# A fused three-layer kernel: full-height first maxima, another order of the maxima in a step, and a PSUM copy moved from ScalarE to VectorE

## The chip, the cores and the metric

The kernel runs on one NeuronCore of a Trainium2 chip as one launch. The metric is the device time of that launch in microseconds. Before the change the median of three runs is 1235.82 us (1234.45 to 1237.55).

## What is computed

Three residual layers on x, of shape 4 x 256 x 256; nearly all of the time goes into the first. It is a cross-attention of x (256 queries a batch) over a context of 4096 rows of 192 values a batch, with 16 heads of 16 columns:

```
q = (layernorm(x) @ Wq + bq)   -> [4, 16 heads, 256, 16]
k = (context @ Wk + bk)        -> [4, 16 heads, 4096, 16]
v = (context @ Wv + bv)        -> [4, 16 heads, 4096, 16]
attn = softmax(clip(q k^T * 16**-0.5, -10000, 10000))
x = x + (attn @ v) @ Wo + bo
```

Then follow a causal self-attention with normed keys and queries, and a layer that routes tokens to 64 slots. Both lie behind the code that the change touches.

## The kernel before, in words

**Groups, steps, units.** The cross-attention runs over 16 groups q of four heads each (four groups a batch). A group has 64 units, one `[128, 512]` PSUM bank each. Four units are a step, one for each head j = 0 to 3, so a group has 16 steps, numbered 0 to 15 here. A unit has two jobs that are far apart in time. Its maximum (`max_unit`, L1708) multiplies a stationary tile of 128 queries by 512 keys, and VectorE reduces the bank to a column (`reduce_unit`, L1173). Its scores (`score_half`, L1722, two products of 256 columns) are key rows by 256 queries; ScalarE takes their exponential (L982). Maxima run AHEAD = 76 units before scores, since the shift of the softmax must be known.

**Split operands.** A product takes only 51 of the array's 128 rows: 16 head columns of keys or queries twice, once more for the low part, and three rows (32 to 34) of ones against the shift in three parts. The even head of a pair lies on partitions 0 to 50 (row half 0), the odd one on 64 to 114 (row half 64). The context's projections in the loop (`passes`, L1674, nine products of 256 columns per half chunk, the first four on row half 64, the last five on row half 0) take 64 rows. Operands on different row halves can be worked on side by side.

**Rings.** Scores use three banks `st` (with two `low` bounds at step 0 and the turned shift behind step 14 in the same ring), maxima use three banks `mxb` (`mx0`, `mx1`, `misc`), with the sums of the last group (`finish`) once a group in the same ring. A user of a ring waits for the release of the user three places before.

**TensorE's order in a step (L1869 on).** Written out by hand: scores of head 0 with two passes, maximum 0, two passes, scores of head 2 with maxima 1 and 2 in and behind them, scores of head 1, a pass, maximum 3, a pass, scores of head 3 with passes. Behind them come, where due, `spread_low` (t = 3), `turn_shift` (t = 59), `values` (L1762: 16 products of 17 columns on four column groups, for the step before), and `finish` (t = 7).

**The other engines' order.** VectorE reduces one maximum a unit; at t = 8 and 9 it takes the reciprocal of the sums and normalises them (`take_sums`, `normalise`); at t = 52 to 60 `shift_step` makes the next group's shift. ScalarE takes one exponential a unit, the bounds at t = 3 (L902), and copies key and value chunks out of `kps`, a half chunk at a time: `k_first_half` (L867), `v_copy_half` (L887), both behind the third exponential of a step; at t = 59 it copies the turned shift (`shift_rows`, L895). POOL splits the context and the keys in two parts (L704, L706, L657, L659), and reads a flag at the head of each group, clears rows of `qst` (L747) and branches; `clip_done`, on which `values` waits, is set behind the branch. SyncE issues the loads of key blocks (L444, L446), queries, context, and the writes of keys.

**The lead.** Before the loop, TensorE computes 20 key chunks and 17 value chunks with full-height products (L1570; 128 rows, then 65 rows), the queries (L1634) and turns of the input (L1622), as 62 `filling`s. Six of them come first, the rest lie between the first 76 maxima, two maxima at a time, with two banks in turn. Keys go through kscr in DRAM: ScalarE copies a chunk, POOL splits it, SyncE writes it, ScalarE's queue loads it back (`load_first`). The rows of ones in the key ring `kst` come from two memsets of VectorE (L1129) and four DMAs of SyncE (`ones_rows`).

```
            for n in range(0, AHEAD, 2):
                max_unit(n)
                max_unit(n + 1)
                filling(fill(n))
                filling(fill(n + 1))
```

Of the kernel before, what the change touches and what calls it, by code (L numbers as in the profile page):

```python
# [31 lines left out]
RB = 12  # L32
NX = 12
# [8 lines left out]
def build(nc, a, out):  # L42

    with ExitStack() as ctx:
# [63 lines left out]

        low = sb("low", [P, 4, T])
# [219 lines left out]
        def fill(m):  # L329

            return m - m // 6 + 6 if m % 6 < 5 else None

        def after_fill(f):

            return f - 6 + (f - 6) // 5 + 2
# [14 lines left out]
        def mx_free(eng, kind, n):  # L350

            place = mx_place[kind, n] - 3 if (kind, n) in mx_place else None
            if place is None:
                wait(eng, max_red, n - 1)
            elif place == -1:
                eng.wait_ge(shift_set, 2)
                eng.wait_ge(flag_abs, 1)
            elif place < 0:
                eng.wait_ge(max_red, AHEAD + place + 2)
            else:  # L360
                user, m = mx_users[place]
                if user == "max":
                    eng.wait_ge(max_red, m + 1)
                else:
                    eng.wait_ge(head_out, 2 * (m + 1))

# [83 lines left out]
        def _(sp):  # L450
# [9 lines left out]
            def ones_rows():  # L460

                sp.wait_ge(ones_set, 2)
                for r in (32, 96):
                    one = kst[r:r + 3, 0:1, 0:512].bitcast(F32)
                    sp.dma_start(kst[r:r + 3, 0, 512:RB * 512].bitcast(F32).rearrange("p (n q) -> p n q", q=512),
                                 one.to_broadcast([3, RB - 1, 512])).then_inc(ones_set, 16)
                    sp.dma_start(kst[r:r + 3, 1, :].bitcast(F32).rearrange("p (n q) -> p n q", q=512),
                                 one.to_broadcast([3, RB, 512])).then_inc(ones_set, 16)

# [39 lines left out]
            def load_q(q):  # L509
# [4 lines left out]
                if 1 <= q < 3:  # L514
                    sp.wait_ge(qst_in, 64 * q)
# [15 lines left out]
            ones_rows()  # L531
# [3 lines left out]
            write_k(2)  # L535
            load_q(0)
# [13 lines left out]
            sp.wait_ge(stacks_in[3], 128)  # L550
            for n in range(8, 10):
                load_block(n)
# [81 lines left out]
        def _(pool):  # L634
# [103 lines left out]
            for q in range(NQ):  # L738
                pool.wait_ge(flag_set, q + 1)
                clipping = pool.value_load(flag[0:1, 0:1])  # L740
                if q > 0 and q + 2 < NQ:
# [6 lines left out]
                    pool.wait_ge(zero_set, 2 * q)  # L748
# [78 lines left out]
        def _(act):  # L827
# [93 lines left out]
            def load_first(n):  # L921

                act.wait_ge(*written(2 * n))
# [45 lines left out]
            act.wait_ge(rows_set, 8)  # L969
# [7 lines left out]
            for n in range(NU):  # L977
# [10 lines left out]
                if t % 4 == 2:  # L988
# [135 lines left out]
        def _(dve):  # L1124
# [3 lines left out]
            for r in (32, 96):  # L1128
                dve.memset(kst[r:r + 3, 0, 0:512].bitcast(F32), 1.0).then_inc(ones_set, 1)  # L1129
# [3 lines left out]
            dve.wait_ge(rows_set, 4)  # L1133
# [32 lines left out]
            def reduce_unit(n):  # L1166
# [5 lines left out]
                at = mxp[:, q % 2, m % 4, m % 8 // 4, m // 8:m // 8 + 1]  # L1172
                dve.reduce_max(at, bank_of_max(n)[:, :], AX.X).then_inc(max_red, 1)  # L1173

            def shift_step(q, t):
# [26 lines left out]
                elif t == 59:  # L1202
# [4 lines left out]
                elif t == 60:  # L1207
# [27 lines left out]

            def sums(q):
# [78 lines left out]
            for n in range(NU):  # L1315
# [245 lines left out]
        def _(pe):  # L1561
# [134 lines left out]
            def max_unit(n):  # L1696

                q, m = n // UQ, n % UQ
                if m == 0:
                    pe.wait_ge(qst_in, 64 * (q + 1))  # L1700
                    if q > 2:
                        pe.wait_ge(zero_set, 2 * (q - 2))
# [3 lines left out]
                j, qt, at = m % 4, m % 8 // 4, n // 8 % RB * 512  # L1706
# [147 lines left out]
            for f in range(6):  # L1854
                filling(f)
            pe.wait_ge(rows_set, 8)
            pe.wait_ge(ones_set, 2 + 16 * 4)
# [413 lines left out]
```

## Time and profile before

| | |
|---|---|
| runs, median | 1235.82 us |
| the profiled execution, its own time | 1235.44 us |
| its span, first to last instruction | 1233.7 us |
| mean granted TensorE clock | 0.935 |
| busy: TensorE / VectorE / ScalarE / POOL | 89% / 64% / 61% / 30% |
| chain that ended last: TensorE / VectorE / ScalarE | 64% / 18% / 5% |

The 1.7 us between own time and span lie outside the instructions. The clock is given as a share of 2.4 GHz; 0.50 is 1.2 GHz. Busy shares overlap and are means over stages: the lead (0 to 156 us), the loop (156 to some 1050 us) and the two later layers (to the end).

### The profile page before, as it was taken

What the parts mean: (1) busy time and instruction counts of PE and PEld (TensorE: products, weight loads), DVE (VectorE), ACT (ScalarE), POOL (GpSimd) and SP (SyncE); (2) the same over time, 40 slices, a digit from 0 to 9 for tenths busy, and PEclk for the clock granted to TensorE, in tenths of its full rate; (3) what the DMA queues carried; (4) which work ended last, traced back from release to release, by engine and by line L of the source; (5) the groups of instructions that cost most, each with busy time, mean ns of one, the idle gap of its engine ahead of it and who ended that gap; (6) DMA issues with size and microseconds to landing.
All of it is one profiled execution on the core that took longest, in us unless ns stands there. A gap on an engine that the chain in (4) does not pass through costs nothing.

```text
span 1233.7 us, 29233 instructions
## 1 busy us (share of the span) xinstructions
PE 1099.1 (89%) x11517; PEld 709.2 (57%) x11521; DVE 791.7 (64%) x1499; ACT 750.1 (61%) x1429; POOL 373.6 (30%) x438
## 2 busy tenths in 40 slices
PE   7899888899898989989898988989889888987997
PEld 6566465565565556555555655555555554555655
DVE  3334577577777877777787777766776612594553
ACT  2111278587777878777787877765766746324432
POOL 4422355344444444444344433140000000202320
PEclk9658899899999999999999999987997989998999
DMA  8731654344454445445444444222342000000001
GB/s 205 233 111 42 190 170 144 116 141 144 128 159 135 135 141 147 134 142 150 132 145 130 148 143 120 63 66 74 104 125 58 25 27 2 1 1 2 3 1 35
DMA packets 117032, 128.66 MB, mean 104 GB/s; under 512 B 19955, under 2 KB 91126, under 8 KB 116864
## 3 DMA queue, kind: packets, MB, share of 16 engines
q1 hardware_dynamic: 111392, 120.29, 33.0%
q10 hardware_dynamic: 5472, 6.23, 2.1%
q8 instruction: 93, 1.52, 0.5%
q14 instruction: 75, 0.61, 0.2%
HBM read 88.42 MB, written 37.75 MB: 102 GB/s over the span
## 4 chain that ended last, share of the span: by engine, by line
PE 64%; DVE 18%; issue 9%; ACT 5%; DMA 2%; SPq 1%; ACTq 0%; POOLq 0%; POOL 0%; DVEq 0%
PE acc L1762 19%; DVE mxp L1173 12%; PE st L1722 12%; PE mx L1708 9%; PE misc L1708 4%; PE st L1570 3%; PE kps L1674 2%; DVE free_k L1408 2%; PE acc L1570 2%; ACT prob L982 1%; PE setB L2022 1%; PE kps L1570 1%; ACT prob L1070 1%; DMA kscr<-o_sb 1%; PE mx L1565 1%
## 5 line engine op out<-in xcount | busy, mean ns | idle before, releaser
L1173 DVE TENSOR_REDUCE mxp<-mx 128x1 f32<-128x512 f32 x709 | 465.6, 683 | 219.4 <-PE mx L1708 219.4
L982 ACT ACTIVATE prob<-st 128x512 f32<-128x512 f32 x704 | 385.7, 598 | 157.9 <-PE st L1722 157.1
L1722 PE MATMUL st<-qst,kst 51*128 51x256 f32 x2048 | 398.1, 304 | 9.1 <-ACT prob L982 8.8
L1722 PEld LDWEIGHTS st<-qst,kst 51*128 51x128 f32 x2048 | 316.0, 192 | 127.0 <-issue 76.8
L1708 PE MATMUL mx<-kst,qst 51*128 51x512 f32 x709 | 282.0, 457 | 47.5 <-DVE mxp L1173 31.5
L1173 DVE TENSOR_REDUCE mxp<-misc 128x1 f32<-128x512 f32 x315 | 215.1, 683 | 64.2 <-PE misc L1708 64.2
L982 ACT ACTIVATE xn<-st 128x512 f32<-128x512 f32 x320 | 176.5, 598 | 56.4 <-PE st L1722 55.7
L1762 PE MATMUL acc<-prob,v_raw 128*17 128x256 f32 x2816 | 196.2, 398 | 9.4 <-issue 5.4
L1708 PEld LDWEIGHTS mx<-kst,qst 51*128 51x128 f32 x709 | 131.3, 194 | 114.3 <-DVE mxp L1173 85.0
L1708 PE MATMUL misc<-kst,qst 51*128 51x512 f32 x315 | 137.6, 437 | 22.8 <-DVE mxp L1173 14.9
L1674 PE MATMUL kps<-w_hi,ctx_p 64*128 64x256 f32 x564 | 153.5, 315 | 0.0
L1674 PE MATMUL kps<-ctx_p,w_hi 64*128 64x256 f32 x528 | 144.5, 314 | 5.9 <-POOL ctx_p L706 5.9
L706 POOL TENSOR_TENSOR ctx_p<-ctx,ctx_p 128x512 fp32r<-128x512 f32 x91 | 116.8, 1284 | 7.3
L1762 PEld LDWEIGHTS acc<-prob,v_raw 128*17 128x17 f32 x2816 | 67.8, 98 | 71.5 <-issue 14.2
L704 POOL CAST ctx_p<-ctx 128x512 fp32r<-128x512 f32 x91 | 55.5, 610 | 146.6 <-PE kps L1674 146.5
L1674 PEld LDWEIGHTS kps<-w_hi,ctx_p 64*128 64x128 f32 x564 | 99.0, 188 | 0.0
L657 POOL CAST kraw<-kraw 128x512 fp32r<-128x512 f32 x50 | 30.6, 612 | 220.9 <-ACT kraw L867 196.6
L1674 PEld LDWEIGHTS kps<-ctx_p,w_hi 64*128 64x128 f32 x528 | 91.4, 186 | 6.2 <-POOL ctx_p L706 6.2
L1762 PE MATMUL acc<-xn,v_raw 128*17 128x256 f32 x1280 | 87.4, 391 | 1.8 <-ACT prob L982 1.4
L1708 PEld LDWEIGHTS misc<-kst,qst 51*128 51x128 f32 x315 | 59.7, 189 | 46.5 <-DVE mxp L1173 38.1
L1674 PE MATMUL kps<-w_lo,ctx_p 64*128 64x256 f32 x282 | 76.3, 284 | 0.0
L1674 PE MATMUL kps<-ctx_p,w_lo 64*128 64x256 f32 x264 | 70.0, 279 | 0.0
(424 smaller groups left out, 1256.5 us busy)
## 6 DMA issues: line engine op xcount, KB each, us to landing
kst<-kscr SPq DMA_DIRECT2D x240, 128.0 KB, 2.5
kscr<-kraw SPq DMA_DIRECT2D x100, 256.0 KB, 2.6
kst<-kscr SPq DMA_DIRECT2D x240, 64.0 KB, 2.6
ctx<-in_ctxT SPq DMA_DIRECT2D x93, 128.0 KB, 2.6
ctx<-in_ctxT SPq DMA_DIRECT2D x184, 64.0 KB, 2.4
kscr<-prob SPq DMA_DIRECT2D x16, 256.0 KB, 3.6
kscr<-o_sb SPq DMA_DIRECT2D x12, 256.0 KB, 4.1
qscr<-v_raw SPq DMA_DIRECT2D x8, 256.0 KB, 2.5
```

The lines of the kernel that those rows point to most:

```text
L657: pool.tensor_copy(first.bitcast(F32R), full).then_inc(k_1, 1)
L704: pool.tensor_copy(hi, raw).then_inc(part_step, 1)
L706: pool.tensor_tensor(lo, raw, hi.bitcast(F32), ALU.subtract).then_inc(part_step, 1)
L982: act.activation(exps(unit_at(n)), st_bank("scores", unit_at(n))[:, :], ACT.Exp).then_inc(exp_done, 1)
L1070: act.activation(pexp[n % 3], setB[:, :, 0:3 * P], ACT.Exp).then_inc(a_exp, 1)
L1173: dve.reduce_max(at, bank_of_max(n)[:, :], AX.X).then_inc(max_red, 1)
L1408: dve.tensor_reduce(amax[:, 2 * b + qt, :, r], bank[:, :, qt * P:(2 * qt + 1) * P], AX.X, ALU.max, negate=True).then_inc(a_max, 1)
L1570: return pe.matmul(to, weights, moving, start=start, stop=stop)
L1674: mm = pe.matmul(kps[:, g * CH:(g + 1) * CH], ctx_part[:, col] if m else w_part[:, col], w_part if m else ctx_part, start=(i == 0), stop=( ...
L1708: pe.matmul(bank_of_max(n)[:, :], qst[row, 2 * (q % 3) + j // 2, qt * P:(qt + 1) * P], kst[row, j // 2, at:at + 512], start=True, stop=Tru ...
L1722: mm = pe.matmul(st_bank("scores", n)[:, h * T:(h + 1) * T], kst[row, j // 2, at:at + P], qst[row, 2 * (q % 3) + j // 2, :], start=True, s ...
L1762: mm = pe.matmul(acc[32 * j:32 * j + VW, 0:T], v4[:, q // 4 % 2 * 32 + n, h, :], exps(UQ * q + 4 * (n // 2) + j)[:, n % 2 * T:(n % 2 + 1) ...
```

## The change

It has these parts:

- **First maxima.** The 64 maxima of group 0 multiply a new tile `qz` (four heads, each on its own rows, zeros on all others) by all 128 rows of the key ring, instead of 51 rows by 51. SyncE loads `qz` with four DMAs ahead of `load_q(0)`; the first maximum waits for both. All rows 32 to 63 and 96 to 127 of the ring are set to one by memsets: four of VectorE in two parts, two of POOL behind key chunk 7. The four DMAs and two small memsets of before are gone; `load_first` waits for the memsets.
- **Fillings.** Eight instead of six come before the first maximum.
- **Order of a step.** The first maximum comes first, the second behind the scores of head 0 and a pass, the third between the halves of head 1, the fourth behind the scores of head 3. The maxima take the heads in the order 1, 0, 2, 3.
- **Value copies.** VectorE makes the second half's copy of each value chunk of the loop, at t % 8 = 6 behind its reduction; ScalarE keeps the first.
- **Ends of groups.** `values` comes ahead of `turn_shift`; `shift_rows` moves to t = 60, behind that exponential, the flag's two steps to t = 60 and 61; `take_sums` and `normalise` both to t = 7.

```diff
@@ helpers @@
+            return (1, 0, 2, 3)[m % 4]          (head_of_max)
@@ sync, behind write_k(2) @@
+            sp.wait_ge(qscr_w, 64)
+            sp.wait_ge(rows_set, 5)
+            for e in range(2):
+                heads_of = qz[:, :, :].rearrange("p (i e) t -> p i e t", e=2)[:, :, e, :]
+                sp.dma_start(heads_of[64 * e:64 * e + 32, :, :].bitcast(F32), ...)
+                sp.dma_start(heads_of[64 * e + 35:64 * e + HR, :, :].bitcast(F32), ...)
             load_q(0)
@@ gpsimd @@
                 k_split(c)
+                if c == 7:
+                    pool.wait_ge(k_2, 8)
+                    for r in (32, 96):
+                        pool.memset(kst[r:r + 32, :, 8 * 512:RB * 512].bitcast(F32), 1.0).then_inc(zero_set, 1)
+                    pool.wait_ge(zero_set, 2)
@@ scalar @@
-                    if c is not None:
-                        v_copy_half(c, t % 8 // 4)
-                if t == 59 and q + 1 < NQ:
+                    if c is not None and t % 8 < 4:
+                        v_copy_half(c, 0)
+                if t == 60 and q + 1 < NQ:
                     shift_rows(q + 1)
@@ vector @@
+            dve.memset(qz[:, :, :].bitcast(F32), 0.0).then_inc(rows_set, 1)
+            def ones_rows(first, end):
+
+                for r in (32, 96):
+                    dve.memset(kst[r:r + 32, :, first * 512:end * 512].bitcast(F32), 1.0).then_inc(ones_set, 1)
...
+            ones_rows(0, 4)
             dve.wait_ge(q_1, 1)
             dve.tensor_tensor(q_sb[:, :, 0:T], ...).then_inc(q_2, 1)
+            ones_rows(4, 8)
...
+                if t % 8 == 6 and v_job(q, t // 8) is not None:
+                    v_copy_half(v_job(q, t // 8))
-                if t == 8 and q > 0:
+                if t == 7 and q > 0:
                     take_sums(q - 1)
-                if t == 9 and q > 0:
                     normalise(q - 1)
@@ tensor, max_unit @@
+                if n < UQ:
+                    pe.matmul(bank_of_max(n)[:, :], qz[:, j, qt * P:(qt + 1) * P], kst[:, j // 2, at:at + 512],
+                              start=True, stop=True).then_inc(max_ps, 1)
+                    return
@@ tensor, a step @@
+                    if more:
+                        max_unit(n + AHEAD)
                     score_half(n, 0)
-                    next(some, None)
                     score_half(n, 1)
                     next(some, None)
                     if more:
-                        max_unit(n + AHEAD)
+                        max_unit(n + 1 + AHEAD)
                     next(some, None)
                     next(some, None)
                     score_half(n + 2, 0)
-                    if more:
-                        max_unit(n + 1 + AHEAD)
+                    next(some, None)
                     score_half(n + 2, 1)
+                    score_half(n + 1, 0)
                     if more:
                         max_unit(n + 2 + AHEAD)
-                    score_half(n + 1, 0)
                     score_half(n + 1, 1)
+                    next(some, None)
+                    score_half(n + 3, 0)
+                    next(some, None)
+                    score_half(n + 3, 1)
                     next(some, None)
                     if more:
                         max_unit(n + 3 + AHEAD)
                     next(some, None)
-                    score_half(n + 3, 0)
-                    next(some, None)
-                    next(some, None)
-                    score_half(n + 3, 1)
                     next(some, None)
...
+                if n >= 7 and t % 4 == 3:
+                    values((n - 7) // UQ, (n - 7) % UQ // 4)
                 if t == 59 and q + 1 < NQ:
                     turn_shift(q + 1)
-                if n >= 7 and t % 4 == 3:
-                    values((n - 7) // UQ, (n - 7) % UQ // 4)
```

## Rows read from the trace of the kernel before

**Rows 1.** Chain that ended last, a steady step: start us, us, engine and line

```profile
503.96 0.70 DVE mxp L1173
...
504.70 0.39 PE mx L1708
...
505.44 0.99 PE acc L1762 x16
...
508.62 0.99 PE acc L1762 x16
```

**Rows 2.** Timeline, the same step: start us, us, engine, instruction, [idle before <-releaser]

```profile
503.18 0.39 PE L1722 MATMUL st<-qst,kst 51*128 51x256 f32 x1
503.40 0.28 PE L1722 MATMUL st<-qst,kst 51*128 51x256 f32 x1
503.52 0.40 PE L1708 MATMUL mx<-kst,qst 51*128 51x512 f32 x1
503.72 1.59 ACT L982 ACTIVATE prob<-st 128x512 f32<-128x512 f32 x3 [0.54 <-PE st L1722]
505.16 0.28 PE L1674 MATMUL kps<-ctx_p,w_lo 64*128 64x256 f32 x1
505.37 1.06 PE L1762 MATMUL acc<-prob,v_raw 128*17 128x256 f32 x16
505.88 0.59 ACT L982 ACTIVATE prob<-st 128x512 f32<-128x512 f32 x1
```

**Rows 3.** Timeline, the step behind `finish`

```profile
551.55 0.35 DVE L1252 TENSOR_TENSOR o_sb<-mx,rcp 128x64 f32<-128x64 f32 x2
551.95 0.50 PE L1708 MATMUL mx<-kst,qst 51*128 51x512 f32 x1 [1.48 <-DVE o_sb L1252]
551.95 0.50 PE L1722 MATMUL st<-qst,kst 51*128 51x256 f32 x2
```

**Rows 4.** Timeline, the products of `finish` in five groups

```profile
493.45 0.63 PE L1565 MATMUL mx<-ident,accs 128*32 128x128 f32 x16
548.94 0.52 PE L1565 MATMUL mx<-ident,accs 128*32 128x128 f32 x12
602.72 0.64 PE L1565 MATMUL misc<-ident,accs 128*32 128x128 f32 x16
821.26 0.62 PE L1565 MATMUL mx<-ident,accs 128*32 128x128 f32 x16
883.30 0.62 PE L1565 MATMUL mx<-ident,accs 128*32 128x128 f32 x16
```

**Rows 5.** Busy time in stretches: last three columns clock, DMA share, GB/s

```profile
45.00:104.00 59.00, 59.00 (x141) 37.42 (x141) 22.89 (x37) 7.98 (x14) 14.20 (x15) 0.50 0.37 114
106.00:141.00 35.00, 34.51 (x143) 22.97 (x142) 19.62 (x31) 9.74 (x17) 9.25 (x13) 1.00 0.36 101
```

**Rows 6.** Chain that ended last, in the lead, before the clock rose

```profile
99.38 3.71 PE misc L1634 x8
103.09 1.65 PE st L1622 x8
```

**Rows 7.** Timeline, the end of a group

```profile
538.14 1.20 ACT L895 ACTIVATE qst<-st 3x512 fp32r<-3x512 f32 x2
...
541.08 0.61 POOL L704 CAST ctx_p<-ctx 128x512 fp32r<-128x512 f32 x1 [2.51 <-PE kps L1674]
```

**Rows 8.** Timeline, the next group's first `values`

```profile
548.08 1.06 PE L1762 MATMUL acc<-prob,v_raw 128*17 128x256 f32 x16 [0.43 <-ACT xn L982]
```

**Rows 9.** Groups by line: VectorE's copies of a full bank out of PSUM

```profile
L1163 DVE COPY xnT<-st x2: 681/681/681, 95.6 to 113.3; 128x512 f32<-128x512 f32 x2
```

**Rows 10.** Timeline, memsets and the queue's issues in the lead

```profile
6.29 1.34 DVE L1136 MEMSET qst<- 3x1536 f32 x1 [0.27 <-issue]
...
19.77 0.69 DVE L1261 TENSOR_TENSOR v_raw<-v_raw 128x512 f32<-128x512 f32 x1 [8.42 <-ACT v_raw L937]
...
30.41 0.42 SPq L517 DMA_DIRECT2D qst<-qscr  x1
...
42.22 2.90 PE L1570 MATMUL acc<-v_raw,wk 128*128 128x256 f32 x8 [1.79 <-ACT prob L859]
```

More of the change, by code:

```diff
@@ L32 @@
 RB = 12
+F0 = 8
 NX = 12
@@ L107, in ctx_of @@
             return ctx4[:, late_slot[c], :, :]
+        first_q = ctx.enter_context(ExitStack())
+        qz = first_q.enter_context(nc.sbuf_tensor("qz", [P, 4, T], F32R))
+        first_q.close()
         low = sb("low", [P, 4, T])
@@ L329, in fill @@
         def fill(m):
-            return m - m // 6 + 6 if m % 6 < 5 else None
+            return m - m // 6 + F0 if m % 6 < 5 else None
         def after_fill(f):
-            return f - 6 + (f - 6) // 5 + 2
+            return f - F0 + (f - F0) // 5 + 2
         def bank_of_max(n):
@@ L365, in mx_free, with head_of_max @@
                     eng.wait_ge(head_out, 2 * (m + 1))
+        def head_of_max(m):
+            return (1, 0, 2, 3)[m % 4]
         def unit_at(n):
@@ L458, in load_early @@
                              a["ctxT"][first:end, P:C, :].rearrange("c p t -> p c t")).then_inc(ctx_in[n], 16)
[L460 to L468, printed above, removed]
             def load_ctx(slot, c):
@@ L514, in load_q @@
                 if 1 <= q < 3:
-                    sp.wait_ge(qst_in, 64 * q)
+                    sp.wait_ge(qst_in, 64 * (q + 1))
                 for e in range(2):
@@ L530, in _ @@
             load_early(4, 8, 3)
-            ones_rows()
             write_k(0)
@@ L535, in _ @@
             write_k(2)
+            sp.wait_ge(qscr_w, 64)
+            sp.wait_ge(rows_set, 5)
+            for e in range(2):
+                heads_of = qz[:, :, :].rearrange("p (i e) t -> p i e t", e=2)[:, :, e, :]
+                sp.dma_start(heads_of[64 * e:64 * e + 32, :, :].bitcast(F32),
+                             qscr1[0:64, :, 0:T].rearrange("(i e d) r t -> e (d r) i t", i=2, e=2)[e]).then_inc(qst_in, 16)
+                sp.dma_start(heads_of[64 * e + 35:64 * e + HR, :, :].bitcast(F32),
+                             qscr2[0:64, 0:T].rearrange("(i e d) t -> e d i t", i=2, e=2)[e]).then_inc(qst_in, 16)
             load_q(0)
@@ L550, in _ @@
             sp.wait_ge(stacks_in[3], 128)
+            sp.wait_ge(zero_set, 2)
             for n in range(8, 10):
@@ L747, in _ @@
                         pool.memset(qst[r:r + 3, to:to + 2, :].bitcast(F32), 0.0).then_inc(zero_set, 1)
-                    pool.wait_ge(zero_set, 2 * q)
+                    pool.wait_ge(zero_set, 2 + 2 * q)
                 with pool.If(clipping != 0):
@@ L921, in load_first @@
             def load_first(n):
+                act.wait_ge(ones_set, 2 if n < 4 else 4)
                 act.wait_ge(*written(2 * n))
@@ L968, in _ @@
                 k_first(c)
-            act.wait_ge(rows_set, 8)
+            act.wait_ge(rows_set, 9)
             shift_rows(0)
@@ L1127, in _ @@
             dve.memset(early[C2:C2 + 1, 0:3, CH:2 * CH], 1.0).then_inc(rows_set, 1)
-            for r in (32, 96):
-                dve.memset(kst[r:r + 3, 0, 0:512].bitcast(F32), 1.0).then_inc(ones_set, 1)
             dve.memset(wv[C2:C2 + 1, 1, :], 0.0).then_inc(rows_set, 1)
+            dve.memset(qz[:, :, :].bitcast(F32), 0.0).then_inc(rows_set, 1)
             dve.memset(shrow[:, :].bitcast(F32), 0.0).then_inc(rows_set, 1)
             dve.memset(spad[:, :, :, :], 0.0).then_inc(rows_set, 1)
-            dve.wait_ge(rows_set, 4)
+            dve.wait_ge(rows_set, 5)
             for r in (32, 96):
@@ L1171, in reduce_unit @@
                 dve.wait_ge(max_ps, n + 1)
-                at = mxp[:, q % 2, m % 4, m % 8 // 4, m // 8:m // 8 + 1]
+                at = mxp[:, q % 2, head_of_max(m), m % 8 // 4, m // 8:m // 8 + 1]
                 dve.reduce_max(at, bank_of_max(n)[:, :], AX.X).then_inc(max_red, 1)
@@ L1201, in shift_step @@
                                       ALU.subtract).then_inc(m_3, 1)
-                elif t == 59:
+                elif t == 60:
                     dve.wait_ge(shift_ps, q + 1)
@@ L1206, in shift_step @@
                                       apply_absolute_value=True).then_inc(flag_abs, 1)
-                elif t == 60:
+                elif t == 61:
                     dve.wait_ge(flag_abs, q + 1)
@@ L1234, in centre_weights, with v_copy_half @@
                                          ALU.mult, ALU.add).then_inc(kq_c, 1)
+            def v_copy_half(c):
+                dve.wait_ge(v_ps, v_steps(c) + 2)
+                dve.wait_ge(v_out, v_steps(c) + 1)
+                if c >= 32:
+                    dve.wait_ge(pv_done, 16 * (4 * (c // 16 - 1) - 1) + c % 16 + 1)
+                dve.tensor_copy(v4[:, 2 * c % 64 + 1, :, 0:DH], kps[:, D:2 * D].rearrange(
+                    "p (h d) -> p h d", d=DH)).then_inc(v_out, 1)
             def sums(q):
@@ L1699, in max_unit @@
                 if m == 0:
-                    pe.wait_ge(qst_in, 64 * (q + 1))
+                    pe.wait_ge(qst_in, 64 * (q + 2))
                     if q > 2:
-                        pe.wait_ge(zero_set, 2 * (q - 2))
+                        pe.wait_ge(zero_set, 2 + 2 * (q - 2))
                 if n % 8 == 0:
@@ L1705, in max_unit @@
                 mx_free(pe, "max", n)
-                j, qt, at = m % 4, m % 8 // 4, n // 8 % RB * 512
+                j, qt, at = head_of_max(m), m % 8 // 4, n // 8 % RB * 512
+                if n < UQ:
+                    pe.matmul(bank_of_max(n)[:, :], qz[:, j, qt * P:(qt + 1) * P], kst[:, j // 2, at:at + 512],
+                              start=True, stop=True).then_inc(max_ps, 1)
+                    return
                 row = slice(64 * (j % 2), 64 * (j % 2) + HR)
@@ L1852, in filling @@
                     early_k(16 + (f - 54) // 2, f % 2)
-            for f in range(6):
+            for f in range(F0):
                 filling(f)
-            pe.wait_ge(rows_set, 8)
-            pe.wait_ge(ones_set, 2 + 16 * 4)
+            pe.wait_ge(rows_set, 9)
             for n in range(0, AHEAD, 2):
```

## The prediction, as put on record before the run

> **What bounds the kernel now.** I read the chain of waits first, since the shares of busy time say little: TensorE is 89% busy, but not at its peak. In a steady step of the loop the chain goes through one reduction of VectorE and the maximum that it releases, then through the products of `values` [rows 1]: VectorE reduces the step's first maximum (0.70 us), only then is a bank free for the fourth (504.70), and `values` ends the step. `values` recurs after 3.18 us [rows 1], mostly 3.17, and does so in 10 or 11 of the 16 steps of every group. The loop is thus held by a round trip, not by an engine: four reductions of 0.68 us a step leave VectorE idle.
>
> The timeline of the same step gives what a forecast needs [rows 2]. I set the step's start at 0 (503.18). The second half of the first scores starts at 0.22, the first maximum at 0.34; other products follow each other on their row half at 0.12 us for 256 columns, 0.23 for 512. ScalarE starts 0.32 after the second half of the scores started, and takes 0.60 for one exponential. `values` starts 0.21 behind the last pass, and the next step 0.99 behind that.
>
> Two more things stand out. Behind `finish`, a maximum waits 1.48 us for the sums to be normalised [rows 3]. And the granted clock is at its low level (0.50, 1.2 GHz) in most of the lead, from 45 to 104 us, with TensorE busy all the time: 0.42 us an instruction there, 0.24 in the stretch behind it with the same mix at 2.4 GHz [rows 5]. The last thing before it rose was the queries and turns, all on 128 rows, 5.4 us without a maximum between [rows 6]; the rounds before, with 51-row maxima and 65-row products in between, had left it low.
>
> **The steady step, worked out again with the new order.** Start 0: first maximum (row half 64) beside the first scores (row half 0). The trace has such a pair, both starting at 551.95 [rows 3]. Second half of the scores 0.22; pass and second maximum 0.34; passes 0.46, 0.57; scores of head 2 0.57 and 0.69; head 1 0.81, with the third maximum beside it, and 0.92; a pass 1.04. The first half of head 3 needs the bank of the first scores: exponential from 0.54 (0.22 + 0.32) to 1.14, release at 1.19 (the row of a released maximum shows 0.04 us). So it starts at 1.19, not 1.04; its second half, after a stop, 0.22 later, at 1.41; fourth maximum 1.53 (its bank is free at 1.27: the first maximum lands at 0.49, reduction to 1.22); last pass 1.64; `values` 1.85; next step 2.84. That is 0.33 less than 3.17. VectorE needs four starts at 0.60, 2.4 us, and ScalarE's last exponential ends 1.31 behind the last pass started (the distance of 505.16 to 506.47 in [rows 2]), at 2.95, before the next step's first scores are there (3.38). The batches without projections have the same path and get the same.
>
> The copy on VectorE, 256 columns from PSUM: bounds are 0.17 (64 columns, half of the pair of 0.35, [rows 3]) and 0.68 (a copy of 512 columns, [rows 9]). I take 0.4, between the ends by its columns. It falls between the third and fourth reduction of one step in four and fills idle time of VectorE (2.8 of 2.84 us then); cover gone, it costs what it takes over, at most 0.3 us on 47 steps, 14 us. What it relieves on ScalarE was hidden.
>
> **Group by group.** From one `finish` to the next is 53.78 us where the clock stays up (548.94 to 602.72, [rows 4]).
> - Ten full steps at -0.33: -3.3.
> - The step behind `finish`: VectorE now has reciprocal and both products (about 0.6 us) right behind the sums, and the third maximum, which uses their bank, comes at 0.81. The 1.48 goes, and a little more: -1.6.
> - Step 13 gains 0.4, step 14 0.3: VectorE's seven small operations of the shift (about 1.4 us in two steps) now delay it.
> - Step 15 loses. The third scores use the bank of the turned shift. Before, ScalarE copied it (1.20 us, [rows 7]) ahead of the step's exponentials, and nothing stood. Now the copy is queued behind the first exponential (ends 1.14), so it ends at 2.36 and the third scores start at 2.41 instead of 0.81. `values` comes at 3.41: +1.4.
> - Steps 0 and 1: nothing. From the last pass of step 15, POOL splits a chunk (541.08, [rows 7]), loads the flag, clears rows and branches, which no busy row shows, and `values` of step 1 waits for it to 548.08 [rows 7, 8]. These 7.0 us hold before and after the change; TensorE's own work in that stretch is some tenths shorter by the distances above (two steps and the two bounds).
>
> Sum: -3.3 - 1.6 - 0.7 + 1.4 = -4.2 a group. Fifteen groups have it (the last has no maxima): -62, with the first, which has no `finish`, 1.6 less: -61.
>
> **Low clock inside the loop.** Groups with such an episode are longer: 55.49 (493.45 to 548.94, [rows 4]), one of five by about 1.7 us, and two of the later ones without projections by about 8: 62.04 (821.26 to 883.30, [rows 4]). Together some 24 us. They began right behind the 1.48 us stop at `finish`. That stop goes, but step 15 gets one as long (0.97 to 2.41, last product landed to next start). So I let three quarters of them stay: -6.
>
> **The lead.** A maximum costs TensorE the same with 51 rows as with 128, if columns set it as they do for the projections' 128 and 65 rows. What can change is the clock. With 128-row maxima no product in these rounds is lower than 65 rows. I expect the clock to rise some ten us into the rounds, at 55 instead of 104. 49 us at 0.42 an instruction become 29 at 0.245 [rows 5]: -20. The bounds are 0 (as before) and -25 (up at once).
> The Trainium skill (TensorE: Matmul & The Clock Gate, Part 1) lets the clock follow how busy the engine has been. The trace disagrees: 59.00 of 59.00 us busy at 0.50. By that rule alone the rows would change nothing, which is the first rival.
>
> Against it: SyncE issues four more loads ahead of `write_k(3)`, 1.9 us at 0.42 each [rows 10], and ScalarE's queue, then chunk 7's copy, then the filling at 42.22 [rows 10] wait for that write: +2. The two fillings moved ahead only move the stop there. Memsets: by 1.34 us for 1536 columns VectorE needs 14 us for 4 x 4096; half of it falls where it was idle for 8.42 us [rows 10], half between that product and the statistics of the other tokens, with some us to spare. POOL needs, at the same rate, 7 us behind chunk 7, which delays chunks 8 and 9, first read by the 33rd maximum. Both at nothing; cover gone, 7 us. SyncE loses four DMAs ahead of its first write, at most 0.4. So the lead gives -18.
>
> **Sum.** -61 - 6 - 18 = -85. The profiled execution's own time is 1235.4 (1.7 over its span), the median 1235.8; so 1151.
>
> **Rivals.**
> 1. The lead's clock stays low (the rows don't matter). For: nothing in the trace shows a 128-row maximum. The loop's gain stays: 1235.8 - 67 + 2 = 1171.
> 2. Another wait takes the reduction's place. The exponential's round trip already is the next limit (1.19 against 1.04). If ScalarE or VectorE is late by some tenths a step (the value copy, an exponential that starts behind its predecessor), the step is 3.0 and the group's gain halves: -32 - 3 - 18, 1183.
> 3. Slower: the maximum at the head of the step, and the one at its end, do not run beside products of the other row half, since nothing in the trace shows one right behind `values` or right ahead of it. Then the first scores start 0.34 later and the passes behind the fourth maximum 0.22: step 3.40, +0.23 each. A group gets 11 x 0.23 - 1.5 + 1.6 = +2.6, fifteen +39; with the lead's -18, 1257. It decides from a step of 3.3 us on. Against: [rows 3], both starting at once.
>
> **Chances.** Forecast (1125 to 1168) 0.50, rival 1 0.22, rival 2 0.20, rival 3 0.08, of which some 0.03 end within 0.3% (what a measurement of this kernel can tell from no change). The forecast's low end is all of the low-clock episodes gone (-18 more) and the lead at its -25. The range goes to 1198, past rivals 1 and 2 and a value copy without cover. Faster 0.92, same 0.03, slower 0.05.
>
> **What would show it.** Right: `values` every 2.84 us in steady steps, with idle time ahead of the fourth scores released by ScalarE, none ahead of the fourth maximum; no wait on the normalising; in step 15 the third scores 1.6 us late behind L895's copy; `finish` to `finish` 49.6 us; clock 1.00 from about 55 us, and the first `values` at about 144 instead of 162 us. Wrong: a step near 3.2 with first scores behind the first maximum; 0.50 up to 100 us; or `kps` passes late behind VectorE's copy.

## The result, and the profile of the changed kernel

Four runs of the changed kernel gave a median of 1132.93 us (1130.69 to 1140.26), four of the kernel before beside them 1235.13 (1227.62 to 1237.55): ratio 0.9192, 95% interval 0.9135 to 0.9250. The profiled execution took 1132.47, span 1130.7, so 103 us less than the profiled one of before, where 85 were forecast. Some executions of any version run at a lower clock and take some per cent longer; the ranges below include them, the ratios don't.

The page of the changed kernel: TensorE's busy share has risen from 89% to 92%, and the row of its granted clock has fewer dents. Section 5 has a new wait, of `scores` for the shift copy; maxima hardly wait for VectorE.

```profile
PE 1043.2 (92%) x11521; PEld 718.0 (63%) x11521; DVE 825.7 (73%) x1549; ACT 712.5 (63%) x1382; POOL 380.7 (34%) x440
...
PEclk9899599999999999999999999979999899999999
...
L1754 PE MATMUL st<-qst,kst 51*128 51x256 f32 x2048 | 409.9, 311 | 31.5 <-ACT qst L906 22.4
...
L1740 PE MATMUL mx<-kst,qst 51*128 51x512 f32 x645 | 267.8, 436 | 1.8 <-DVE mxp L1189 1.5
```

**A steady step.** Timeline of the changed kernel, against [rows 2]. L1740 is the maximum, L1754 the scores, L1702 the passes, L1794 `values`, L994 the exponential, L1258 the new copy on VectorE.

```profile
496.70 0.50 PE L1740 MATMUL misc<-kst,qst 51*128 51x512 f32 x1
496.70 0.50 PE L1754 MATMUL st<-qst,kst 51*128 51x256 f32 x2
...
497.04 0.39 PE L1740 MATMUL mx<-kst,qst 51*128 51x512 f32 x1
...
497.93 0.39 PE L1754 MATMUL st<-qst,kst 51*128 51x256 f32 x1
...
498.27 0.39 PE L1740 MATMUL misc<-kst,qst 51*128 51x512 f32 x1
...
498.60 1.06 PE L1794 MATMUL acc<-prob,v_raw 128*17 128x256 f32 x16
499.58 0.50 PE L1740 MATMUL mx<-kst,qst 51*128 51x512 f32 x1
```
```profile
497.28 2.06 ACT L994 ACTIVATE prob<-st 128x512 f32<-128x512 f32 x4 [0.54 <-PE st L1754]
```
```profile
499.04 0.41 DVE L1258 COPY v_raw<-kps 128x256 f32<-128x256 f32 x1
```

The first maximum and the first scores start together at 496.70. The fourth scores start 1.23 later (forecast 1.19), their second half and the fourth maximum follow at once, `values` comes at 1.90 (1.85), the next step at 2.88 (2.84). It was 3.17. The new copy falls into idle time of VectorE, 0.41 us at 499.04.

**Behind `finish`** (L1593) nothing stops, and from one `finish` to the next are 49.82 us, against 53.78 in [rows 4]:

```profile
493.25 0.63 PE L1593 MATMUL mx<-ident,accs 128*32 128x128 f32 x16
493.82 0.49 PE L1740 MATMUL mx<-kst,qst 51*128 51x512 f32 x1
...
543.07 0.64 PE L1593 MATMUL misc<-ident,accs 128*32 128x128 f32 x16
```

**Step 15** has the new wait. First exponential, shift copy (L906), and only then the third scores, 2.45 behind the step's start at 531.54:

```profile
531.54 0.50 PE L1754 MATMUL st<-qst,kst 51*128 51x256 f32 x2
532.12 0.60 ACT L994 ACTIVATE prob<-st 128x512 f32<-128x512 f32 x1 [0.76 <-PE st L1754]
532.74 1.20 ACT L906 ACTIVATE qst<-st 3x512 fp32r<-3x512 f32 x2
533.99 0.38 PE L1754 MATMUL st<-qst,kst 51*128 51x256 f32 x1 [1.47 <-ACT qst L906]
```

**The lead.** Busy time in stretches (columns as in [rows 5]), then the chain in a cycle of rounds:

```profile
38.90:45.70 6.80, 6.18 (x15) 4.94 (x16) 1.29 (x2) 2.06 (x4) 6.07 (x4) 0.50 1.03 270
45.70:114.00 68.30, 64.66 (x292) 51.91 (x290) 44.90 (x73) 17.74 (x31) 30.43 (x32) 1.00 0.52 152
114.00:137.90 23.90, 18.12 (x93) 11.58 (x95) 13.83 (x28) 8.89 (x17) 13.07 (x15) 0.50 0.68 211
```
```profile
49.82 0.86 PE kps L1598 x4
50.68 0.87 PE acc L1598 x4
51.55 0.47 PE mx L1736 x2
...
54.02 0.69 DVE mxp L1189
```

The clock rises at 45.7 instead of 104. At the end of the lead, where TensorE has stops (18.12 us busy of 23.90), it falls again, from 114.0 to 137.9; before, it did so for 13.7 us from 145.5. The first `values` start at 134.2 (before 162.4). VectorE's reduction is on the chain in the rounds here, as it was not between 43 and 104 us before: with the clock up, TensorE catches up with the two-bank ring.

### The profile page after: what moved, and what is told of

Read it like the earlier page. It is cut to its first block, busy times and chain, and to the rows that moved or that the text cites. A ratio compares the mean times of both kernels' runs of the same rounds, so it can differ in the third digit from the quotient of the medians.

```text
span 1130.7 us, 29261 instructions
## 1 busy us (share of the span) xinstructions
PE 1043.2 (92%) x11521; PEld 718.0 (63%) x11521; DVE 825.7 (73%) x1549; ACT 712.5 (63%) x1382; POOL 380.7 (34%) x440
## 4 chain that ended last, share of the span: by engine, by line
PE 76%; issue 7%; DVE 7%; ACT 7%; DMA 1%; POOL 1%; SPq 1%; ACTq 0%; POOLq 0%; DVEq 0%
PE acc L1794 21%; PE st L1754 16%; PE mx L1740 9%; PE kps L1702 8%; PE misc L1740 5%; DVE free_k L1436 2%; PE st L1598 2%; ACT prob L994 2%; ACT qst L906 1%; PE mx L1736 1%; PE setB L2053 1%; ACT prob L1082 1%; DVE mxp L1189 1%; PE acc L1598 1%; PE mx L1593 1%
## 5 line engine op out<-in xcount | busy, mean ns | idle before, releaser
L994 ACT ACTIVATE prob<-st 128x512 f32<-128x512 f32 x704 | 377.1, 600 | 152.7 <-PE st L1754 152.2
L1754 PE MATMUL st<-qst,kst 51*128 51x256 f32 x2048 | 409.9, 311 | 31.5 <-ACT qst L906 22.4
L1754 PEld LDWEIGHTS st<-qst,kst 51*128 51x128 f32 x2048 | 299.4, 190 | 66.9 <-ACT qst L906 25.5
L1740 PE MATMUL mx<-kst,qst 51*128 51x512 f32 x645 | 267.8, 436 | 1.8 <-DVE mxp L1189 1.5
L994 ACT ACTIVATE xn<-st 128x512 f32<-128x512 f32 x320 | 172.2, 600 | 56.8 <-PE st L1754 56.4
L1794 PE MATMUL acc<-prob,v_raw 128*17 128x256 f32 x2816 | 193.9, 394 | 9.2 <-issue 5.4
L1740 PEld LDWEIGHTS mx<-kst,qst 51*128 51x128 f32 x645 | 122.9, 191 | 69.1 <-issue 35.9
L1740 PE MATMUL misc<-kst,qst 51*128 51x512 f32 x315 | 135.6, 430 | 0.0
L1702 PE MATMUL kps<-ctx_p,w_hi 64*128 64x256 f32 x528 | 129.2, 311 | 4.9 <-POOL ctx_p L717 4.9
L1702 PE MATMUL kps<-w_hi,ctx_p 64*128 64x256 f32 x564 | 132.5, 301 | 0.0
L1794 PEld LDWEIGHTS acc<-prob,v_raw 128*17 128x17 f32 x2816 | 66.1, 98 | 75.7 <-issue 12.7
L1702 PEld LDWEIGHTS kps<-w_hi,ctx_p 64*128 64x128 f32 x564 | 104.7, 186 | 2.1
L1702 PEld LDWEIGHTS kps<-ctx_p,w_hi 64*128 64x128 f32 x528 | 100.7, 192 | 7.3 <-POOL ctx_p L717 5.2
L1794 PE MATMUL acc<-xn,v_raw 128*17 128x256 f32 x1280 | 85.5, 385 | 2.1 <-ACT prob L994 2.1
L1740 PEld LDWEIGHTS misc<-kst,qst 51*128 51x128 f32 x315 | 59.4, 189 | 32.8 <-issue 16.2
L1702 PE MATMUL kps<-w_lo,ctx_p 64*128 64x256 f32 x282 | 74.4, 278 | 0.0
L1702 PE MATMUL kps<-ctx_p,w_lo 64*128 64x256 f32 x264 | 71.0, 283 | 0.0
```

What stands on the lines that cost most here:

```text
L994: act.activation(exps(unit_at(n)), st_bank("scores", unit_at(n))[:, :], ACT.Exp).then_inc(exp_done, 1)
L1702: mm = pe.matmul(kps[:, g * CH:(g + 1) * CH], ctx_part[:, col] if m else w_part[:, col], w_part if m else ctx_part, start=(i == 0), stop=( ...
L1740: pe.matmul(bank_of_max(n)[:, :], qst[row, 2 * (q % 3) + j // 2, qt * P:(qt + 1) * P], kst[row, j // 2, at:at + 512], start=True, stop=Tru ...
L1754: mm = pe.matmul(st_bank("scores", n)[:, h * T:(h + 1) * T], kst[row, j // 2, at:at + P], qst[row, 2 * (q % 3) + j // 2, :], start=True, s ...
L1794: mm = pe.matmul(acc[32 * j:32 * j + VW, 0:T], v4[:, q // 4 % 2 * 32 + n, h, :], exps(UQ * q + 4 * (n // 2) + j)[:, n % 2 * T:(n % 2 + 1) ...
```

## The experiments

Five questions: what in the lead makes the 28 us, what the order of the steps is worth, what step 15's wait costs, whether the copy on VectorE gains anything, and whether the exponential's round trip really sets the step. The kernel before ran beside each set of kernels: 1230.08 us for the first, 1237.15 for the second, 1239.19 for the third.

**1. The rows alone: first maxima back to 51 rows.**

```diff
-                if n < UQ:
-                    pe.matmul(bank_of_max(n)[:, :], qz[:, j, qt * P:(qt + 1) * P], ...)
-                    return
```

> The changed kernel, but its first 64 maxima multiply 51 rows by 51 again (the loads of qz, the memsets and the eight fillings stay). Theory (the array's height in use decides over the clock in the lead, and a change between 51-row and 128-row products costs TensorE some 0.2 us each way round): the clock stays at 0.50 up to about 100 us, the first values move from 134 back to about 160 us, time about 1160. Rival (the rows do nothing, the lead was shortened by the fillings and by the DMAs that went): first values at about 136, time within 3 us of 1133. Second rival (clock not touched, only the changes between heights cost): low stretch as short as now, first values 5 us later, 1138.

Measured: 1162.16 us (1157.96 to 1170.15), ratio 0.9452 (0.9367 to 0.9537). The first `values` are back at 161.1, so the rows carry 27 of the lead's 28 us. Busy time in two stretches, and a cycle of the lead at full clock:

```profile
39.30:93.90 54.60, 53.58 (x125) 33.73 (x126) 20.16 (x32) 8.15 (x14) 23.89 (x20) 0.50 0.46 142
```
```profile
116.97 0.50 PE L1736 MATMUL mx<-kst,qst 51*128 51x512 f32 x2
117.40 2.00 PE L1598 MATMUL st<-wv,v_raw 128*128 128x256 f32 x8
119.33 0.51 PE L1736 MATMUL mx<-kst,qst 51*128 51x512 f32 x2
...
123.58 0.50 PE L1736 MATMUL mx<-kst,qst 51*128 51x512 f32 x2
```

TensorE is busy 53.58 of 54.60 us and stays at 0.50 (1.2 GHz); with 128-row maxima in the same places it rose at 45.7. The second fence shows what I had not seen: between two pairs of 51-row maxima, eight filling products take from 117.40 to 119.33, 1.93 us. Eight filling products take 0.86 + 0.87 = 1.73 in the changed kernel (chain above, also at full clock). Six maxima with their twenty filling products take 6.61 here (116.97 to 123.58) and 6.04 there (61.84 to 67.88). So 128 rows are cheaper even where the clock is the same. Two things change together in this experiment: the rows of the maxima, and the changes between heights that 51-row maxima bring. The runs do not tell which of the two kept the clock low.

```profile
61.84 0.50 PE L1736 MATMUL mx<-kst,qz 128*128 128x512 f32 x1
```

The Trainium skill (TensorEngine Tiling (Array Packing), Key Properties) says that a change of tiling mode drains TensorE. The trace agrees, with the 0.2 us above; that it is a drain is the page's word, and the runs show only that the time goes where the heights change.

**2. Only the first sixteen maxima on 128 rows.**

```diff
-                if n < UQ:
+                if n < 16:
```

> The changed kernel with 128-row products for the first 16 maxima only, the other 48 of group 0 on 51 rows. Theory (full height is needed to raise the clock, not to hold it: the kernel of before held 1.00 from 105 us on with 51-row maxima; and every change between the heights costs about 0.2 us): the low stretch ends at about 46 us as in the changed kernel and does not come back before the last maxima; eight cycles of six maxima cost 0.55 more each, first values at about 138, time about 1137. Rival (full height is also needed to hold it): the clock falls again at some 60 us, first values above 150, time above 1148.

Measured: 1150.52 us (1135.82 to 1181.43), ratio 0.9292 (0.9067 to 0.9518). First `values` at 141.2, 7 later than with all 64. The clock was up through the 51-row maxima that followed:

```profile
62.00:119.00 57.00, 56.15 (x237) 37.47 (x236) 33.01 (x52) 14.76 (x26) 19.18 (x23) 1.00 0.46 136
```

So 16 maxima on 128 rows were enough for the rise here, and the 51-row maxima behind them did not end it. (Between 50.7 and 54.1, still among the sixteen, the clock was low once more, behind a stop of 2.41 us.) The 48 other maxima pay by the height changes: 48 / 6 x 0.57 = 4.6 of the 7 us. The time is further off than 7 us because two late groups of this profiled run had 17 and 31 us of low clock (from 743.6 and 798.2 on), which the lead's rows don't touch.

**3. Six fillings ahead instead of eight.**

```diff
-F0 = 8
+F0 = 6
```

> The changed kernel with six fillings ahead of the maxima, as before the change. Theory (TensorE stands ahead of the filling of chunk 9 whatever was put in front of it, as ScalarE's queue waits for a key write): first values within 2 us of 134, time 1133 to 1136. Rival (the two fillings ahead keep the clock up or shorten the lead): a longer low stretch and first values at 138 or later, 1138 and up.

Measured: 1137.08 us (1129.75 to 1151.98), ratio 0.9226 (0.9085 to 0.9366), first `values` at 135.6 against 134.2. The two fillings move a stop and save nothing that can be measured.

**4. The order alone, in the kernel before** (order of a step and of the heads in it, nothing else).

```diff
+                    if more:
+                        max_unit(n + AHEAD)
                     score_half(n, 0)
-                    next(some, None)
...
```

> The kernel of before with the new order of a step and of the heads, nothing else. Theory: steady steps of 2.88, the stop behind finish stays at about 1.5 us, the end of a group costs what it did, lead as before (first values at 162): 1235 - 48 = about 1187, give or take 6 for stretches of low clock. Rival (VectorE's copy and the order need each other): steps of 3.0 or more, 1205 and up.

Measured: 1160.44 us (1158.83 to 1165.46), ratio 0.9425 (0.9353 to 0.9498): 27 us better than expected. Steady steps are 2.88, so the order makes the whole of that gain. The step behind `finish` stays at 4.65, as it must with the sums taken a unit later; step 14 is 3.72 and step 15 2.93, 0.9 less than the changed kernel's 2.88 + 4.68. A group takes 50.4, 3.4 less than before: 51 us in fifteen. The first `values` come 4 us earlier (158.2). The rest, some 15 us, fits the low clock: 131 us of it in the whole profiled run where before had 162, and at half speed the difference is 15. I had priced only the steps.

**5. The old order, in the changed kernel.**

```diff
-                    if more:
-                        max_unit(n + AHEAD)
                     score_half(n, 0)
+                    next(some, None)
...
```

> The changed kernel with the step's order of before (maxima between, heads 0, 1, 2, 3); all else as changed. Theory (a step was held by the round trip first maximum, reduction, fourth maximum): steady steps go back from 2.88 to 3.17 us, 11 in each of 15 groups, +48: about 1181, and the wait of the fourth maximum for the reduction is back. The lead stays at 134 us. Rival (the order is worth little, the moved copy of values and the ends of groups freed the step): steps below 3.0, time below 1150.

Measured: 1193.48 us (1185.76 to 1201.27), ratio 0.9677 (0.9596 to 0.9758). Steady steps 3.17, first `values` at 135.9. Step 15 is 4.51, so its loss belongs to ScalarE's new queue order and not to the step's. The timeline shows the reduction's wait again, in each steady step:

```profile
496.69 0.49 PE L1740 MATMUL misc<-kst,qst 51*128 51x512 f32 x1 [0.19 <-DVE mxp L1189]
```

The median lies 12 us above the expected 1181. I had counted the steady steps alone: with those behind `finish` and at the end, a group is 3.6 us longer by its steps, 54 in fifteen. The low clock of its profiled run adds up to 107 us where the changed kernel has 77, which is 15 at half speed. Together that is 69, and the two profiled runs lie 69 apart (1201.27 and 1132.47).

**6. The shift copy one unit earlier on ScalarE.**

```diff
-                if t == 60 and q + 1 < NQ:
+                if t == 59 and q + 1 < NQ:
                     shift_rows(q + 1)
```

> The changed kernel with ScalarE's copy of the turned shift one exponential earlier, at t = 59 as before the change; values stay ahead of the turn. Theory (step 15 stands because that copy is queued behind the first exponential): the third scores of step 15 start at about 1.3 instead of 2.4 us, but the first exponential is 0.7 later and the fourth scores wait for it: step 15 from 4.68 to about 3.9, 15 times, -12: about 1121, with fewer stretches of low clock. Rival (ScalarE now stands waiting for the turn, which values precede, and holds the exponential of head 3 and the next step): no gain or a loss, 1130 to 1145.

Measured: 1115.53 us (1109.79 to 1119.00), ratio 0.9074 (0.9004 to 0.9145); once more, on another chip:

> shift_copy_t59 once more, on the same chip as turn_first_early, since the two are to be compared: step 15 at 3.86, about 1116 us. If it comes out within 0.3% of turn_first_early, the turn's place is worth nothing beside the copy's.

1115.79 us (1108.72 to 1120.56), ratio 0.9069 (0.8989 to 0.9149). The ten runs of the two lie below all four of the changed kernel. Step 15 in the timeline:

```profile
523.78 0.50 PE L1754 MATMUL st<-qst,kst 51*128 51x256 f32 x2
523.88 1.21 ACT L906 ACTIVATE qst<-st 3x512 fp32r<-3x512 f32 x2 [0.30 <-PE st L1767]
525.33 0.35 PE L1754 MATMUL st<-qst,kst 51*128 51x256 f32 x1 [0.58 <-DVE flagf L1221]
```

The third scores start 1.55 behind the step's start instead of 2.45. They wait for the copy and for VectorE's flag reduction, which reads the same bank. The step is 3.86 instead of 4.68; 0.8 x 15 is 12 us, and 17 were gained: the low clock in its first profiled run adds up to 39 us against 77 (in the other run to 77 as well). Only the part between the first `values` and the last group can come from step 15: there it is 8 and 23 us in these two runs and 38 in the changed kernel. Over all profiled runs with the stop of step 15 in them (the changed kernel, 1, 2, 3, 5, 8 and 9) it is 28 to 85 us there; in the four with the copy at t = 59 (these two and those of experiment 7) it is 7 to 23. This version beats both kernels.

**7. The turn of the shift ahead of the last `values`, too.**

```diff
-                if n >= 7 and t % 4 == 3:
-                    values((n - 7) // UQ, (n - 7) % UQ // 4)
                 if t == 59 and q + 1 < NQ:
                     turn_shift(q + 1)
+                if n >= 7 and t % 4 == 3:
+                    values((n - 7) // UQ, (n - 7) % UQ // 4)
```

> The changed kernel with the turn of the shift ahead of values and its copy at t = 59 again, as before the change. Theory (step 15 pays the queued copy, step 14 the wait for VectorE's small operations; with the new order and the old end, steps 14 and 15 took 3.73 + 2.93 against 2.88 + 4.68 now): -0.9 in 11 groups, -1.4 in the four without projections, and fewer stretches of low clock, about 1116, level with the copy at t = 59 alone. Rival (VectorE, which has the value copy as well now, makes the shift later): step 14 above 4.2, 1123 or more.

Measured: 1118.86 us (1118.09 to 1126.54), ratio 0.9095 (0.8975 to 0.9214). Step 14 is 3.72 and step 15 3.60, together 0.6 more than in 6 (2.88 + 3.86). Would it pay if VectorE's small operations came earlier?

```diff
-                    shift_step(q + 1, t)
+                    if t == 53:
+                        shift_step(q + 1, 53)
+                    if 53 <= t < 57 or t in (59, 60):
+                        shift_step(q + 1, t + 1)
+                    elif t == 52:
+                        shift_step(q + 1, 52)
```

> The kernel after, with the turn of the shift ahead of the last values of step 14, ScalarE's shift copy a unit earlier (t=59), and VectorE's seven small operations of the shift up to one unit earlier (the last from t=54 to 60, the flag at t=59 and 60). Theory: in turn_first_t59 steps 14 and 15 were 3.72 and 3.6 us because TensorE and the third scores waited for VectorE's small operations, not for the turn's place. With them earlier, step 14 is some 3.1 (no wait, 0.2 for the shift's products) and step 15 some 2.93 (as in order_alone), against 2.88 + 4.68 in the kernel after and 2.88 + 3.86 in shift_copy_t59: -1.5 a group against after, about 1109 us. Rival: VectorE has no room for them earlier either and delays the maxima of steps 13 and 14: the two steps stay at some 7.3 together, about 1116.

Measured: 1118.08 us (1114.58 to 1121.47), ratio 0.9108 (0.9035 to 0.9182), beside 1115.79 for the copy's move alone. The two steps are 3.90 + 3.52, so the rival's outcome came. Timeline of step 14, the fourth maximum waiting for the reduction that stands behind a small operation:

```profile
276.37 1.28 POOL L665 TENSOR_TENSOR kraw<-kraw 128x512 f32<-128x512 f32 x1
...
276.84 0.86 DVE L1211 SCALAR_TENSOR_TENSOR spad<-sres 128x8 bf16<-128x8 f32 x1
...
277.60 0.68 DVE L1189 TENSOR_REDUCE mxp<-mx 128x1 f32<-128x512 f32 x1
...
278.33 0.50 PE L1745 MATMUL mx<-kst,qst 51*128 51x512 f32 x1 [0.52 <-DVE mxp L1189]
```

The small operation, on 128x8 values, takes 0.86 us, where the same line takes 0.18 at its shortest, and it ends 0.05 behind POOL's split of the keys (276.37 + 1.28). That is no chance: in the profiled runs of this variant and of experiment 9, 51 small operations of the shift took over 0.25 us, every one ended 0.02 to 0.06 behind an operation of POOL, and none of the short ones lay inside an operation of POOL. Where only one of them met POOL (the group that begins at 388.9), step 14 was 3.29, and in the three groups from 685.6 on, where none of them did, 2.98 to 3.06. So it is less the seven operations' own time that VectorE has no room for than the time in which they wait for POOL.

**8. All value copies back on ScalarE.**

```diff
-                    if c is not None and t % 8 < 4:
-                        v_copy_half(c, 0)
+                    if c is not None:
+                        v_copy_half(c, t % 8 // 4)
```

> The changed kernel with ScalarE copying both halves of each value chunk again. Theory (ScalarE's last exponential ends before the next step's first scores are there, with or without the copy): steady steps stay at 2.88, time 1131 to 1135. Rival (the copy would delay the exponential of head 3 and the next step): one step in four at 3.0 or more, 47 of them, 1139 or more.

Measured: 1144.20 us (1135.89 to 1184.76), ratio 0.9303 (0.9069 to 0.9538). Every steady step is 2.88, first `values` at 135.0. Its best two runs, 1135.89 and 1136.41, lie within the changed kernel's range; its median is 11 us higher, which no step explains. The copy's move is worth nothing that the steps show.

**9. A shorter first exponential** (this kernel leaves out half of the first exponentials).

```diff
-                act.activation(exps(unit_at(n)), st_bank("scores", unit_at(n))[:, :], ...)
+                w = 256 if n % 4 == 0 else 512
+                act.activation(exps(unit_at(n))[:, 0:w], st_bank("scores", unit_at(n))[:, 0:w], ...)
```

> The kernel after, with the exponential of each step's first scores over 256 of its 512 columns (half of these exponentials is left out). Theory: the steady step of 2.88 us is set by the fourth scores, which start 1.23 behind the step's start when the first exponential has freed their bank; a half exponential frees it some 0.25 us earlier, TensorE then gets to them at 1.04, the step is some 2.70, a group 2 us shorter, about 1105 us. Rival: the step is set elsewhere (VectorE's four reductions, 0.70 each with their starts, 2.8 us a step): it stays at 2.85 or more and the time within 0.5% of the kernel after's.

Measured: 1120.48 us (1116.90 to 1123.44), ratio 0.9122 (0.9012 to 0.9231). Steady steps are 2.79 to 2.81 where a projection runs beside them, and 2.69 to 2.70 in the last groups, which have none. Timeline of a step with projections:

```profile
253.71 0.50 PE L1741 MATMUL mx<-kst,qst 51*128 51x512 f32 x1
253.72 0.50 PE L1755 MATMUL st<-qst,kst 51*128 51x256 f32 x2
...
254.77 0.36 PE L1755 MATMUL st<-qst,kst 51*128 51x256 f32 x1
...
255.52 1.06 PE L1795 MATMUL acc<-prob,v_raw 128*17 128x256 f32 x16
```

The fourth scores now start 1.06 behind the step's start: the exponential did hold them. `values` comes at 1.81, 0.09 earlier, and not 0.18: behind the fourth scores TensorE now works without a stop; without projections `values` waits for the last exponential:

```profile
759.79 0.56 PEld L1795 LDWEIGHTS acc<-prob,v_raw 128*17 128x17 f32 x16 [0.24 <-ACT prob L995]
```

But the group gains only some 0.5 us (49.3 against 49.8), since steps 14 and 15 are 3.91 + 4.50 instead of 2.88 + 4.68. With steps of 2.79, VectorE's small operations are late, and the fourth maximum of step 14 waits:

```profile
278.40 0.18 DVE L1212 SCALAR_TENSOR_TENSOR spad<-sres 128x8 bf16<-128x8 f32 x1
278.48 0.68 DVE L1190 TENSOR_REDUCE mxp<-mx 128x1 f32<-128x512 f32 x1
278.48 1.28 POOL L717 TENSOR_TENSOR ctx_p<-ctx,ctx_p 128x512 fp32r<-128x512 f32 x1
...
278.53 0.50 PE L1741 MATMUL mx<-kst,qst 51*128 51x512 f32 x1 [0.53 <-DVE mxp L1190]
...
279.08 0.74 DVE L1217 TENSOR_TENSOR spad<-sres,spad 128x8 bf16<-128x8 f32 x1
```

It is POOL again: three of the seven operations of this group took 0.60, 0.85 and 0.74 us (the last one above), each ending 0.02 to 0.06 behind POOL's. In the one group with projections where only one of them was long (the one that begins at 390.2), step 14 took 2.84 instead of 3.91.

The whole came out 15 us above the expected 1105. So a step of the changed kernel has its limits close together: the exponential's round trip at 2.88 and TensorE's own work at 2.79, and in step 14 VectorE's small operations, where they meet POOL's.

## Why the prediction was right, and where its terms were off

The forecast of 1151 stood 18 us above the result, inside its likeliest case (1125 to 1168).

- **Steady step**: 2.88 for 2.84. The mechanism is the one forecast: no wait for the reduction, the fourth scores released by the first exponential. The 0.04 is ScalarE, which starts 0.36 behind the second half of the scores (497.28 behind 496.92) where 0.32 was read from [rows 2]. Experiments 4 and 5 tie it to the order alone, 9 to the exponential.
- **Behind `finish`**: 3.32 for the 3.29 that follow from -1.6. Right.
- **Steps 13 and 14**: both 2.88. I had step 14 at 3.3, delayed by VectorE's backlog. It had just enough room: experiment 9, with steps of 2.79, and 4 and 7, with the turn ahead of `values`, all show step 14 at 3.7 to 3.9 in most groups. The sum priced the seven operations by their own time (1.4 us); what they wait for POOL is in none of its terms.
- **Step 15**: 4.68, forecast 3.2 + 1.4 = 4.6, and by the mechanism forecast. Experiment 6 takes 0.8 of it back.
- **A group**: 49.82 for 49.6. Fifteen groups give -59, and -58 without the 1.6 that the first does not have, where -61 stood. (15 x 4.2 is 63, not the 62 of the sum; less 1.6 it comes to -61 all the same.)
- **Low clock in the loop**: three quarters were to stay. From the first `values` to the last group before had 61 us of it, after 38, so some six tenths. That stretch shrank by 71.5 us (832.1 to 760.7), 58 by the steps and 13.5 beside them, where 6 were forecast; 23 us less of low clock are 12 at half speed. That the stop of step 15 brings the episodes that stay was argued in the forecast, and the runs make it likely: 28 to 85 us of low clock in this stretch with the stop, 7 to 23 without (experiment 6). Why the clock falls behind some of these stops and not behind others stays open.
- **The lead**: the mis-sized term, -28 for -18. The sum read "-20" for the clock, from 49 us at 0.42 an instruction, and "A maximum costs TensorE the same with 51 rows as with 128". The rise came at 45.7 where 55 stood. Low clock ahead of the first `values` fell from 75.1 us (61.4 + 13.7) to 27.0 (6.8, and 20.2 of the stretch that begins at 114.0; the sum had no term for this second one). 48 us at half speed are 24. The rest comes from the sentence on the maximum, which was wrong: by experiment 1, maxima of the fillings' own height cost 0.57 us less for each six with their fillings, 6 for all 64. That makes 30, and the +2 for SyncE's loads would close the sum, but no run shows it (four issues of 0.42 are 1.7 us, not 1.9).
- **The tail**: 3.3 us shorter, with nothing changed in it; it had 12 us of low clock where before had 25.

The other cases did not come. Rival 1 (the rows don't matter) fell with experiment 1. The rule that it took from the Trainium skill (TensorE: Matmul & The Clock Gate, Part 1), that the clock follows how busy TensorE has been, does not come out by the busy time of the profile: 53.58 of 54.60 us busy stayed at 0.50 with 51-row maxima, and 6.18 of 6.80 us busy with 128-row ones were followed by 1.00. Rival 2 (another wait takes the place) is there by 0.04 of a step. Rival 3 is excluded by the pair at 496.70.

## What to carry to other kernels

In a round trip between two engines, write the step out with every release time and look for the second limit. Here it lay 0.29 us behind the first and gave the step to within 0.04. When work is reordered, go through the special steps (end of a group, shift, sums) in each engine's queue: the ordinary steps gained as forecast, and the one place where a copy fell behind an exponential cost 0.8 us a group, mended by one number. When an operation takes several times its usual length, look at what the other engines run beside it: here, VectorE seemed to have no room, and was waiting for POOL. And look at a product whose height differs from its neighbours': here such products cost more than their columns, and the clock stayed low with them.

## What the runs showed of the hardware

- The clock's rise followed the rows of the products: low from 39.3 to 93.9 with maxima on 51 rows, low from 38.9 to 45.7 with 128, the fillings alike. Whether the height counts or the change between heights is not shown. Once up, it stayed up through 51-row maxima (1.00 from 62 to 119 in experiment 2).
- A stretch of eight products of 128 and 65 rows took 1.93 us between 51-row maxima and 1.73 between 128-row ones, both at full clock.
- VectorE's operations on 128x8 values took 0.15 to 0.24 us alone and 0.40 to 0.87 when they met an operation of POOL, ending 0.02 to 0.06 behind it (51 of 51 in experiments 7, second variant, and 9). Its reductions out of PSUM kept their 0.68 beside POOL's work.
- VectorE's copy of 256 columns out of PSUM took 0.41 us, ScalarE's 0.39.
- Low-clock episodes vary from run to run: 39 and 77 us of them (8 and 23 in the loop) in the two profiled runs of experiment 6's kernel, which took 1109.79 and 1120.56 us, on two chips. Differences under 1% were therefore read from the steps, not from the totals.
